# An attention layer on one core: DVE's third group of statistics, and SyncE's stores and loads of x, moved in their orders

## What is computed

```
h = relu(layernorm(x))
q, k, v = h Wq' + bq, h Wk' + bk, h Wv' + bv
a = q k' / 16 + adj + adj
out = x + softmax(a, rows) v
```

## Time and profile before

| | |
|---|---|
| median of three runs | 740.02 us (736.87 to 742.82) |
| the profiled execution | 735.11 us, of which the span of instructions 733.4 us |
| mean granted TensorE clock | 0.984 of full speed |
| PE busy | 693.4 us, 95% of the span, 4799 matmuls |
| of these: weighing (L1442, moving v_sb) | 2796 + 276 = 3072 |
| of these: the seven products (L1503) | 1344 |
| DVE, ACT, POOL busy | 599.9 us (82%), 436.7 (60%), 433.7 (59%) |
| chain that ended last, by engine | PE 50%, DMA 18%, SP's queue 16%, DVE 8% |
| mean DMA rate | 220 GB/s |

### The profile page before, as it was taken

One profiled execution on the slowest core, in us unless ns is written; L12 is line 12 of the kernel. 1 busy time (PEld: TensorE's weight loads), 2 busy tenths in 40 slices (PEclk: granted clock), 3 DMA queues, 4 the chain that ended last, 5 costly groups with the idle time before them and its releaser, 6 DMA issues.

```text
span 733.4 us, 14700 instructions
## 1 busy us (share of the span) xinstructions
PE 693.4 (95%) x4799; PEld 473.1 (65%) x4799; DVE 599.9 (82%) x1282; ACT 436.7 (60%) x732; POOL 433.7 (59%) x436
## 2 busy tenths in 40 slices
PE   5588998999999999999999989999999999999988
PEld 4455554566666676766666756666666666666776
DVE  4889776789797879788888869787877888897996
ACT  3799662675656665656666565656575566656530
POOL 1789602565655657474756555564747475655667
PEclk7699999999999999999999999999999999999999
DMA  8298597998988888899989979899999999998573
GB/s 267 102 264 242 148 225 215 256 239 242 237 217 240 230 224 221 222 220 248 230 230 222 228 207 244 221 228 236 211 229 245 227 224 242 235 228 228 148 179 81
DMA packets 93244, 161.06 MB, mean 220 GB/s; under 512 B 20976, under 2 KB 41840, under 8 KB 93168
## 3 DMA queue, kind: packets, MB, share of 16 engines
q1 hardware_dynamic: 68432, 126.41, 65.7%
q10 hardware_dynamic: 24736, 33.72, 18.8%
HBM read 80.35 MB, written 8.39 MB: 121 GB/s over the span
## 4 chain that ended last, share of the span: by engine, by line
PE 50%; DMA 18%; SPq 16%; DVE 8%; issue 4%; ACT 2%; POOL 1%; ACTq 0%; DVEq 0%; POOLq 0%
PE bank L1442 28%; PE bank L1503 21%; SPq L420 13%; DMA xT<-rows 8%; DMA out_y<-xy 4%; DMA g_pair<-g_scratch 2%; DMA rows<-in_x 2%; SPq L372 1%; DVE rows L1127 1%; DMA v_sb<-xT 1%; DVE rows L1100 1%; SPq L409 1%; DMA rows<-in_adj 1%; DVE stats L1045 1%; DVE top L1136 1%
## 5 line engine op out<-in xcount | busy, mean ns | idle before, releaser
L624 POOL TENSOR_TENSOR wT<-xT,wT 128x512 f16<-128x512 f32 x233 | 268.9, 1165 | 216.7 <-ACT wT L806 213.2
L1442 PE MATMUL bank<-v_sb,wT 128*128 128x256 f16 x2796 | 344.8, 273 | 7.8 <-POOL wT L624 4.5
L1503 PE MATMUL bank<-top,a_op 128*128 128x512 f16 x1344 | 331.5, 380 | 7.3 <-DVE rows L1078 3.5
L1442 PEld LDWEIGHTS bank<-v_sb,wT 128*128 128x128 f16 x2796 | 273.2, 98 | 91.3 <-POOL wT L624 6.5
L806 ACT CAST wT<-xT 128x512 f16<-128x512 f32 x233 | 139.6, 612 | 133.6 <-PE bank L1442 78.0
L1503 PEld LDWEIGHTS bank<-top,a_op 128*128 128x128 f16 x1344 | 130.5, 98 | 118.5 <-DVE rows L1078 5.0
L777 ACT ACTIVATE rows<-rows,exp_bias,exp_scale 128x1024 f32<-128x1024 f32 x128 | 158.7, 1240 | 59.4 <-issue 30.8
L1100 DVE CUSTOM_DVE_ANT_0 rows<-bank,rows 128x512 f32<-128x512 f32 x256 | 173.5, 680 | 10.3 <-PE bank L1503 2.0
L1127 DVE STREAM_TRANSPOSE rows<-rows 128x1024 f32<-128x1024 f32 x128 | 158.3, 1239 | 8.8 <-ACT rows L777 8.7
L1085 DVE SCALAR_TENSOR_TENSOR rows<-rows,adj_scale,bank 128x512 f32<-128x512 f32 x64 | 47.7, 745 | 40.5 <-PE bank L1503 40.5
L1078 DVE SCALAR_TENSOR_TENSOR rows<-rows,adj_scale,bank 128x512 f32<-128x512 f32 x64 | 47.5, 742 | 31.3 <-PE bank L1503 15.7
(11 more groups left out here) (115 smaller groups left out, 479.3 us busy)
## 6 DMA issues: line engine op xcount, KB each, us to landing
rows<-in_adj SPq DMA_DIRECT2D x128, 512.0 KB, 5.7
xT<-rows SPq DMA_DIRECT2D x488, 64.0 KB, 3.8
xT<-rows ACTq DMA_DIRECT2D x488, 64.0 KB, 4.3
rows<-in_x SPq DMA_DIRECT2D x8, 512.0 KB, 6.0
xy<-in_x SPq DMA_DIRECT2D x32, 128.0 KB, 4.7
g_scratch<-xT SPq DMA_DIRECT2D x16, 256.0 KB, 3.1
g_pair<-g_scratch SPq DMA_DIRECT2D x15, 256.0 KB, 5.7
out_y<-xy SPq DMA_DIRECT2D x30, 128.0 KB, 5.4
```

Of the source, the lines that this page charges most:

```text
L624: nc.gpsimd.tensor_tensor(split_piece(m, 1), exchanged(m), split_piece(m, 0), ALU.subtract).then_inc(split_lo, 1)
L1442: return nc.tensor.matmul(out_ap, stationary, moving, start=first, stop=last)
L1503: last = nc.tensor.matmul(ps[:], s, mv, start=first and k == 0, stop=k == 2, skip_group_check=True)
```

## The change

In SP's loop the stores and loads of `xy` change places. The store of the even tile goes from period 4p + 2 to 4p + 3, the store of the odd one from 4p + 3 to 4p + 4; the two loads, which stood together in period 4p + 3 right behind the odd store, go one to period 4p + 4 and one to 4p + 5. The loop is one period longer, for the last store. On DVE `statistics(2)` goes behind `low_key(0, B21)` and the two low halves of the folded weights.

```diff
--- before.py
+++ after.py
@@ -507,13 +507,14 @@
                     exchange_a(u)
                 if unit_in_range(u - 1):
                     refill(u - 1, 1)
-                if n % QUADS in (2, 3) and p >= 2:
-                    store(2 * (p - 2) + n % QUADS - 2)
-                if n % QUADS == 3 and 1 <= p and p + 1 < PAIRS:
-                    load_xy(2 * p + 2)
-                    load_xy(2 * p + 3)
-
-            for n in range(SETUP, PERIODS + WEIGH_LAG + 1):
+                if n % QUADS == 3 and p >= 2:
+                    store(2 * (p - 2))
+                if n % QUADS == 0 and p >= 3:
+                    store(2 * (p - 3) + 1)
+                if n % QUADS in (0, 1) and 2 <= p < PAIRS:
+                    load_xy(2 * p + n % QUADS)
+
+            for n in range(SETUP, PERIODS + WEIGH_LAG + 2):
                 period(n)
             for slot in range(XY):
                 halves = (TILES - 2) % XY == slot or (TILES - 1) % XY == slot
@@ -1264,7 +1265,6 @@
                                            ALU.add).then_inc(folded, 1)
             nc.vector.scalar_tensor_tensor(fold[:, 3], wvT_ps[:, 0, :], wv_scale[:], fold[:, 1],
                                            ALU.mult, ALU.add).then_inc(folded, 1)
-            statistics(2)
             low_key(0, B21)
             dve.wait_ge(weights_hi, 6)
             dve.wait_ge(folded, 2)
@@ -1272,6 +1272,7 @@
                                     ).then_inc(weights_lo, 1)
             nc.vector.tensor_tensor(ws_lo[:], fold[:, 3], ws_hi[:], ALU.subtract
                                     ).then_inc(weights_lo, 1)
+            statistics(2)
             statistics(3)
             statistics(4)
             low_key(0, B22)
```

## The result

Over 20 runs of each kernel the median went from 739.93 us (727.87 to 748.82) to 730.15 us (727.45 to 733.48). The recorded ratio is 0.9936, 95% interval 0.9913 to 0.9959: faster by 0.64%. The two statements differ because the comparison leaves out runs more than 1.5% above their kernel's quickest (above 738.8 us), which are 13 of the 20 runs of the kernel before and none of the changed one. So the change takes away a cost that the kernel before pays in varying size. The forecast was 729.5 us, 1.4% faster.

What follows compares the result with a forecast made beforehand. PE sets the pace until 380 us, then SP's queue, late from waiting on a fresh store, starves it. 735.1 - 7.2 - 1.0 = 726.9; 731.8 if the median's 4.9 us excess stays; middle 729.5, range 723 to 738.

Steps and rivals of the forecast that it cites:

- PE's 7.6 us late in the loop: PE idle from 380 to 680 us, laid to SP's queue; 7.2 us of it forecast to go, bounds 0 and 7.6.
- the return of the exchange's landing wait: On SP, 2.2 us of landing covered by the load's wait may come back; SP's cycle then at most 38.3 us.
- The front: Moving statistics(2) on DVE starts PE 2.3 us earlier; 1.0 us of that gained, bounds -1.3 and 2.3.
- Its length was 1.65 us next to a busy POOL ... I keep 1.65: DVE's low half of B21 moves to 23.72 us and keeps its length, POOL being as busy there.
- nearest to the eviction that releases SP: Front's value taken from ScalarE's second eviction of g, at 33.9 us instead of 34.87: 1.0 us gained.
- The bound of -1.3: Front's worst case: only the delay of POOL's factors of group 2, ending 1.3 us later, carries on.
- ScalarE's waits: In the loop, ScalarE waits 0.9 us for the even load and 0.7 for the odd one, costed at nothing.
- their cover is gone from about 5 us on: ScalarE's waits for `xy` stay free until about 5 us, as its exponential ends 5.6 us before DVE's transpose.
- rival 2: Slower: ScalarE hangs on the loads; landings of 10.3 us would give 760 us; chance 0.06.
- the middle between "goes" (726.9) and "stays" (731.8): The median's 4.9 us above the profiled execution either vanishes as more gaps or stays as an offset; 729.5 taken.
- Rivals 1 and 3: 1: transfers are the limit, 736 us, chance 0.17. 3: exchange's landing takes the wait's place, 739 us, chance 0.07.
- my shortest loop: Load issue, landing, ScalarE's h, split, exponential, DVE's transpose: closes when a load needs over 9.3 us, then 1 us per us.

Runs made afterwards that it cites:

- xy7: The kernel before, both orders untouched, with 7 slots of `xy` instead of 6; 728.32 us, ratio 0.9851.
- odd_later: The kernel before with only the odd load of `xy` moved to the end of SP's next period; 726.99 us, ratio 0.983.
- filler: The changed kernel with 14 unused matmuls on PE between project_g(0, 0) and project_g(0, 1); 731.43 us, ratio 0.9887.
- sp_only: The changed kernel with statistics(2) put back, so only SP's stores and loads moved; 727.44 us, ratio 0.9822.
- loads_late: SP's stores and loads moved, statistics at their old place, and each load one step later still, behind the next refill; 782.59 us, ratio 1.0538.
- after_again: The changed kernel run once more, unedited, as the mark beside the kernel before on the same chip; 729.75 us, ratio 0.9852.

## Why the prediction was right and wrong

**What bounds the kernel: right.** SP ran at 40.5 us per cycle, and took PE's 7.6 us late in the loop. With the wait gone PE idles 0.25 us, and `xy7` and `odd_later` show that the wait for the fresh store was all of it. The cycle is PE's, 39.3 us. I had priced the return of the exchange's landing wait at up to 2.2 us per cycle; in total that wait went from 98.7 to 100.0 us only (71 times instead of 44). The 57 us that SP had spent on the store went into waits for POOL (43.8 us instead of 3.0) and for the transposes (23.4 instead of 6.5), that is, into SP's slack.

**The front: wrong in sign.** I forecast 1.0 us gained; it costs 2.0 us at the mark and 2.3 at the end. The step that failed is "Its length was 1.65 us next to a busy POOL ... I keep 1.65": I priced the low half of B21 beside POOL, and took the two small low halves behind it along at their old 0.41 us. They moved under POOL too and stretched to 1.48 and 1.37. With that the statistics ended not at 28.4 but at 29.9 us, the factors of group 2 at 31.3 instead of 30.1. The path was wrong too. I took the value "nearest to the eviction that releases SP". That way was 1 us late instead of 1 us early (SP's store of g at 36.53 against 35.57), and `filler` gave it all back without moving the mark. What counts is DVE's own order, which runs without idle time up to 39.6 us, and the way over group 4's factors and the query sums behind it. The bound of -1.3 was too narrow for the same reason.

**ScalarE's waits: mis-sized.** Forecast 0.9 and 0.7 us; measured 56.6 / 26 = 2.2. The loads land after 5.6 us (median), not 4.7. Taken load by load, the 4.7 was a mixture: in the kernel before the even load, right behind a refill already, took 5.8 us (median of 14), and the odd one, which went out some 5 us later after its wait, 2.7; in the changed kernel they take 5.6 and 5.5. In both kernels each of the 28 landed at least 0.4 us after the refill ahead of it. For tile 6 the other terms can be read off too: the exchange took 5.78 us instead of 5.1, and refill and store, with the wait ahead of the refill, 1.9 instead of 1.0. In other cycles SP also waits for POOL ahead of the exchange.

That the waits cost nothing was right (`xy7` against `sp_only`), but "their cover is gone from about 5 us on" was somewhat too generous: `loads_late` puts the edge between 2.2 and 4.3 us. That cover, and the loop of rival 2, I had drawn over the exponential and the transpose; in `loads_late` the chain goes over ScalarE's high halves and POOL's low halves, which I had left out. In the changed kernel itself neither cost anything.

**The numbers.** The absolute forecast, 729.5, met 730.15 by luck, by two errors of opposite sign. The excess of the median over the profiled execution did go, so the middle between "goes" (726.9) and "stays" (731.8) put 2.6 us too much on, and the front was 3 us worse than forecast: 726.9 + 3 would have been nearly the same. The change in per cent was forecast against the median of the kernel before, as if it were one value. Its runs spread over 21 us, the changed kernel's over 6; against the part of them in the recorded ratio the gain is 0.64%, in the first group here it is 1.5% (0.9852 for `after_again`). So the term that was mis-sized is the 4.9 us of excess over the profiled execution: it goes, but where it varies from run to run the kernel before also has runs with little of it (its quickest took 727.87 us), and a ratio against those is smaller: the medians differ by 9.8 us, the recorded 0.64% are 4.7. With the front as forecast, 3 us better, it would have been about 1.1%, an estimate from these numbers. That the excess is "more of the same gaps" is not shown, since one execution of that kernel was traced. Forecast with the front's true sign, the profiled execution gives 735.1 - 7.3 + 2 = 729.8, 0.7% faster. Rivals 1 and 3 are out: the transfers keep up (235 and 231 GB/s), and the wait is gone.

## What to carry to other kernels

Look for a wait on a transfer that was issued just ahead on the same in-order queue; here one more buffer or one step of distance removed it, and the least edit that did was enough. Before moving an instruction, look at what its new neighbours on other engines are, for it and for those that move up or back with it: two small ones at 0.41 us each became 2.85 us. And when they have moved, follow the delay along the busiest engine's own queue first. If a load is moved towards its reader, draw the ring all the way round, through every engine that works behind the reader, since here loads that went one step later and landed after 7.0 us cost 2 us each, where my shortest loop had room for 9.3. And where a kernel's runs scatter by 3%, forecast against that spread and not against one median.

## What had not been expected of the hardware

Two DVE subtractions of 128 x 256 with both inputs in SBUF took 0.41 us beside POOL's factors and 1.48 and 1.37 us beside POOL's subtractions of 128 x 512; they ended 0.3 us after the subtraction that they had met. PE's granted clock fell from full to half within its idle stretch from 29.3 to 33.0 us (0.72 on average there, 0.50 after it), and 14 idle matmuls kept it up. The odd 128 KB load of `xy` landed after 2.7 us (median) when it went out some 6 us behind a 512 KB refill, and after 5.5 right behind one; in `loads_late` the median of all was 7.0.
